# FFN1 of a recurrent block: the fetch of W1's blocks moves from SyncE's queue to ScalarE's, and VectorE's transpose of them to the head of its tile

## What is computed

```python
def quant_rows(a):
    scale = jnp.maximum(jnp.max(jnp.abs(a), axis=-1, keepdims=True) / 127.0, 1e-8)
    return jnp.clip(jnp.round(a / scale), -127.0, 127.0) * scale

def linear8bit(x, W, b):
    outlier = jnp.max(jnp.abs(x), axis=(0, 1)) > 3.0
    y = quant_rows(jnp.where(outlier, 0.0, x)) @ quant_rows(W).T
    return y + jnp.where(outlier, x, 0.0) @ W.T + b

xn = layernorm(x)                       # x: 4 x 512 x 512, f32
h = linear8bit(xn, W1, b1)              # W1: 2048 x 512
g = silu(linear8bit(h, W2, b2))         # W2: 512 x 2048
out = x + attention(xn) * g
```

## Time and profile before

| | |
|---|---|
| median of 3 runs | 801.87 us (799.75 to 803.87) |
| profiled execution, its own time | 802.13 us |
| span of its trace | 800.4 us |
| TensorE busy | 756.8 us, 95% |
| VectorE busy | 650.9 us, 81% |
| ScalarE busy | 395.4 us, 49% |
| GpSimd busy | 274.5 us, 34% |
| FFN1 in the trace | from 408.1 to 603.9 us |

### The profile page before, as it was taken

The page is one execution under the profiler, slowest core; times in us unless marked ns, Lnnn a source line. Parts: engine busy times, 40 slices in busy tenths (PEclk is TensorE's granted clock), DMA queues, the critical chain, the costliest instruction groups (busy, mean ns, idle before and its releaser), DMA issues. The chain is left out here.

```text
span 800.4 us, 11979 instructions
## 1 busy us (share of the span) xinstructions
PE 756.8 (95%) x4133; PEld 569.1 (71%) x4133; DVE 650.9 (81%) x1115; ACT 395.4 (49%) x670; POOL 274.5 (34%) x349
## 2 busy tenths in 40 slices
PE   5999999999999999999998998899997999999995
PEld 4878665556776767766576876688886788888884
DVE  7988999999999899995536585686868998599957
ACT  4354167767676667777633354355453333132212
POOL 7213135555555555554622112122200000036504
PEclk9999599999999999999999999999999999999999
DMA  7421303323222223334455857646332778436982
GB/s 265 146 106 53 81 21 89 82 81 95 82 83 83 82 82 100 88 108 134 158 184 141 253 149 180 171 99 149 77 71 73 270 216 263 165 106 219 307 315 105
DMA packets 115276, 110.71 MB, mean 138 GB/s; under 512 B 71808, under 2 KB 71824, under 8 KB 113680
## 3 DMA queue, kind: packets, MB, share of 16 engines
q1 hardware_dynamic: 115216, 109.95, 46.5%
HBM read 56.43 MB, written 40.37 MB: 121 GB/s over the span
## 5 line engine op out<-in xcount | busy, mean ns | idle before, releaser
L933 DVE TENSOR_REDUCE rowmax<-ps 128x2 f32<-128x512 f32 (+3 forms) x384 | 210.4, 591 | 19.6 <-PE ps L1010 18.0
L854 ACT ACTIVATE probs<-ps 128x512 f32<-128x512 f32 (+1 forms) x352 | 174.8, 558 | 71.3 <-PE ps L1023 70.0
L1010 PE MATMUL ps<-km,stack 128*128 128x256 f32 (+3 forms) x512 | 149.7, 347 | 2.2 <-PEq L195 1.9
L1023 PE MATMUL ps<-stack,ks 128*128 128x512 f32 (+1 forms) x352 | 131.4, 383 | 2.8 <-ACT probs L854 2.7
L1010 PEld LDWEIGHTS ps<-km,stack 128*128 128x128 f32 (+1 forms) x512 | 94.2, 197 | 43.2 <-DVE rowmax L933 23.8
L836 POOL TENSOR_SCALAR_AFFINE_SELECT probs<-probs 128x512 f32<-128x512 f32 x128 | 81.0, 641 | 78.3 <-ACT probs L854 77.1
L1861 PE MATMUL ps<-big_h 128*128 128x512 f32 x256 | 99.9, 390 | 2.0 <-issue 1.6
L1863 PE MATMUL ps<-big_h,big_l 128*128 128x512 f32 x256 | 99.6, 389 | 0.0
L1862 PE MATMUL ps<-big_l,big_h 128*128 128x512 f32 x256 | 99.6, 389 | 0.0
L1036 PE MATMUL ps<-probs,vones 128*32 128x512 f32 (+3 forms) x1024 | 82.2, 439 | 0.2 <-POOL probs L836 0.2
L1023 PEld LDWEIGHTS ps<-stack,ks 128*128 128x128 f32 x352 | 66.5, 189 | 11.7 <-ACT probs L854 6.2
(11 more groups left out here) (227 smaller groups left out, 1375.5 us busy)
## 6 DMA issues: line engine op xcount, KB each, us to landing
stack<-big_h SPq DMA_DIRECT2D x128, 64.0 KB, 2.0
h_scratch<-hs SPq DMA_DIRECT2D x7, 1024.0 KB, 4.5
hload<-h_scratch SPq DMA_DIRECT2D x14, 512.0 KB, 5.1
xn_scratch<-xa SPq DMA_DIRECT2D x4, 1024.0 KB, 4.4
stack<-big_l SPq DMA_DIRECT2D x64, 64.0 KB, 2.0
xi<-xn_scratch SPq DMA_DIRECT2D x16, 256.0 KB, 2.7
xe_scratch<-xm SPq DMA_DIRECT2D x16, 256.0 KB, 2.3
w2n<-in_L_ffn_W_dram SPq DMA_DIRECT2D x4, 1024.0 KB, 6.0
```

The costliest lines, as they stand in the source:

```text
L854: nc.scalar.activation(probs[p][:, o:o + nh * w], ps[:, STB[n % NST], 0:nh * w], ACT.Exp).then_inc(s_exp, 1)
L933: nc.vector.tensor_reduce(dst, src, AX_X, ALU.max).then_inc(s_red, 1)
L1010: last = nc.tensor.matmul(dst, stack[u % 3][rows, hp, P * qt:P * (qt + 1)], km[rows, u // KT, p0:p0 + npar, keys], start=True, stop=True)
L1023: ins = nc.tensor.matmul(ps[:, STB[n % NST], 0:nh * w].rearrange("p (h q) -> p h q", h=nh), ks[:, u // KT, p, P * kt:P * (kt + 1)], stack[ ...
```

## The change

Step 5 is issued from ScalarE's program instead of SyncE's: `load_w1_blocks(f + 2)` stands in tile f, behind the eviction of chunk 2 and ahead of that of chunk 3. (Before, SyncE had `load_w1_blocks(f + 1)` at the head of tile f.) Its waits stay the same. VectorE has step 6, `turn_w1(f + 1)`, as the first thing in tile f, ahead of `feature_max(f - 1)` and of step 2. In tile 0 step 2 for tile 2 moves ahead of `low_w1(1)`.

```diff
@@ SyncE @@
-                def load_w1_blocks(f):
-
-                    sp.wait_ge(s_w1k[f % 2], X_LOADED + 16 * (f // 2))
-                    if f > 2:
-                        sp.wait_ge(s_w1u, f - 2)
-                    for a in range(HB):
-                        rows = w1q_d[f % 2, :, :].rearrange("(b j) (k a i) -> a j k b i", b=HB, k=KT, a=HB)[a]
-                        sp.dma_start(w1x[SQ * a:SQ * (a + 1), :].rearrange("j (k b i) -> j k b i", k=KT, b=HB),
-                                     rows).then_inc(s_w1x, 16)
...
                 for f in range(FT):
-                    if 2 <= f + 1 < FT:
-                        load_w1_blocks(f + 1)
                     if f + 3 < FT:
                         load_w1(f + 3)
@@ ScalarE @@
+                def load_w1_blocks(f):
+
+                    act.wait_ge(s_w1k[f % 2], X_LOADED + 16 * (f // 2))
+                    if f > 2:
+                        act.wait_ge(s_w1u, f - 2)
+                    for a in range(HB):
+                        rows = w1q_d[f % 2, :, :].rearrange("(b j) (k a i) -> a j k b i", b=HB, k=KT, a=HB)[a]
+                        act.dma_start(w1x[SQ * a:SQ * (a + 1), :].rearrange("j (k b i) -> j k b i", k=KT, b=HB),
+                                     rows).then_inc(s_w1x, 16)
...
                         if c == 2 and f == 0:
                             high_w1(1)
+                        if c == 2 and f + 2 < FT:
+                            load_w1_blocks(f + 2)
@@ VectorE @@
                     if f == 0:
                         for i in range(EARLY, NT):
                             low_x(i)
+                        scale_w1(2)
                         low_w1(1)
+                    if 2 <= f + 1 < FT:
+                        turn_w1(f + 1)
                     if f:
                         feature_max(f - 1)
-                    if f + 2 < FT:
+                    if f and f + 2 < FT:
                         scale_w1(f + 2)
-                    if 2 <= f + 1 < FT:
-                        turn_w1(f + 1)
```

## The result

The changed kernel took 826.28 us, the median of four runs from 824.16 to 830.33, against 801.69 us before: a ratio of 1.0312, with a 95% interval from 1.0262 to 1.0362. The forecast was 824 us, slower. The profiled execution took 827.42 us, 25.3 more than the profiled one of before, and its span is 825.7 us. FFN1 goes from 408.6 to 629.3 us, 24.9 us longer than before; but for some tenths, the whole loss lies there.

A forecast was written before the change was run, and what follows sets the result against it. A ring longer than TensorE's 11.2 us tile bounds FFN1: from 422.75, thirteen passes of 12.85 us plus 14.2 of W2 traffic, then the last tiles, end FFN1 at 625.65, 21.7 us later: 824 us, range 805 to 843.

The forecast's parts named there:

- The ring: FFN1's loop of fetch, turn, feature maximum, scale, rounding, store, next fetch; one pass per tile, 12.85 us against TensorE's 11.2.
- The holes: TensorE's idle gaps in FFN1, waiting for W1's low part; forecast before nearly each tile through 13, also in 9 to 13.
- The ring without traffic: One pass with nothing beside the fetch: 8.5 us without the fetch, plus 4.35 for it, 12.85 us in all.
- The traffic: W2's stores and loads beside the fetch: 1.0 us in seven passes, 2.4 in three, nothing in three; sum 14.2 us.
- rival 4: Queues take turns: fetch issues wait for SyncE's, W2's load costs what both 1 MB transfers cost; 28 us, 838 us, chance 0.18.
- The end: Tile 14 starts 0.75 us before the last fetch at 604.0; two tiles of 11.2 us follow, FFN1 ends at 625.65.
- a lower clock: TensorE's slower matmuls after each hole, about 1.5 us; said to fall into the ring's slack, except once in tile 14.
- Rival 1: The holes go: TensorE runs 11.2 us tiles, 10.4 to 14 us less, about 790 us; chance 0.08.

## Why the prediction was right

**The mechanism.** The ring was read from the program's order and priced from rows of before; the chain after shows each of its steps. Undoing VectorE's half removes the loss, undoing ScalarE's does not, and 1.2 us more in the ring make the thirteen passes 13.0 us longer. The holes are fewer than forecast: seven, not one ahead of nearly each tile. Behind each of the five longest, 2.6 to 8.7 us, the tile runs at the lower clock at first and takes 12.6 to 13.7 us instead of 11.2, and the tile after it finds its low part ready.

**The ring without traffic.** Forecast 8.5 us without the fetch and 4.35 for it. Measured: 8.41 on the mean of 13 passes, and 4.37 for the fetch in two of the three tiles with no pieces of W2 (5.23 in the third). ScalarE's queue, then VectorE's turns, for a fetch beside W2's load (first row of each) and one beside nothing:

```profile
449.65 3.42 ACTq L1468 DMA_DIRECT2D w_blocks<-w_rounded_scratch  x4
...
468.84 2.63 ACTq L1468 DMA_DIRECT2D w_blocks<-w_rounded_scratch  x4
```

```profile
460.54 0.71 DVE L1558 STREAM_TRANSPOSE w1t_first<-w_blocks 128x512 f32<-128x512 f32 x1 [9.68 <-DMA w_blocks<-w_rounded_scratch]
473.21 0.71 DVE L1558 STREAM_TRANSPOSE w1t_second<-w_blocks 128x512 f32<-128x512 f32 x1 [4.28 <-DMA w_blocks<-w_rounded_scratch]
```

So the issue costs ScalarE what it cost SyncE (2.63 and 2.61 us), and the fetch is not shorter for its move. The Trainium skill ("DMA: Bandwidth & Descriptors", section "Issuing engines are not separate DMA queues") has all queues share the DMA engines; the trace agrees, with 4.37 us measured against 4.35 taken from SyncE's queue, and 7.2 to 10.9 us beside W2's load on the other queue.

**The traffic** is the term that was mis-sized, in both directions. For one or two pieces of W2 beside the fetch I took 1.0 us; seven passes measured 0.45 to 0.6. For W2's load I took 2.4 us, from a fetch in line behind it; the three measured 6.5, 2.8 and 3.8 us, in a queue beside it, the first of them above the upper bound of 4.5. Where I took nothing, one of three measured 0.9. The sum was 17.6 us instead of 14.2; that it is so near is luck in part, as the seven passes gave back 3.5 us of the 5.9 that the three cost more. Of rival 4 the half on W2's load was thus the nearer one (4.5), and the half on turns was not: the fetch's issues stayed at 2.64 us beside eight stores that took 4.93.

**The end** was 1.1 us later than the last fetch gave. Two terms did it together. I priced the low part at 1.27 us, and the one for tile 12 took 3.31 (first row; the last section has more on it), so TensorE starts that tile 2 us late, at 581.83. And I let a lower clock, at 1.5 us, fall into the ring's slack except in tile 14. Tile 12, behind a wait of 5.98 us, takes 13.7 us instead of 11.2; in the stretch where it starts the granted clock is 0.74. TensorE has no hole from there on. Tile 14's low part was ready at 605.60, and the tile starts at 606.75; with either term as forecast it would have started at about 605.7 (an estimate, from 11.2 us for tile 13).

```profile
578.47 3.31 POOL L1408 TENSOR_TENSOR w_low_first<-w1t_first,w_high_first 128x512 fp32r<-128x512 f32 x1
```

```profile
470.10 0.79 PE L1839 MATMUL ps<-big_h,w_high_first 128*128 128x512 f32 x1 [8.66 <-POOL w_low_first L1408]
...
581.83 0.79 PE L1839 MATMUL ps<-big_h,w_high_first 128*128 128x512 f32 x1 [5.98 <-POOL w_low_first L1408]
```

Together 25.3 us in the profiled execution, for 21.7 forecast.

**The rivals.** Rival 1, the holes gone, needed a fetch under 2.7 us; none was under 4.37. But its kernel exists: the change's queue with the old order took 793.8 us, where rival 1 said about 790.

## What to carry to other kernels

When a step that waits is moved ahead in an in-order program, follow what is queued behind it until the path ends or comes back: if it comes back, its length against the tile's length decides, and it is no use that each wait alone has a tile of room. A prefetch is only ahead if the data it fetches are made in an earlier tile than the one that it is issued in. And test the parts of a change one by one: here one half alone gained 1%, and the other alone lost 7.8%.

## What the runs showed of the hardware

GpSimd's low part, 128 x 512, took 1.27 to 1.31 us before and 3.31 in seven of its 14 places in the change, where it starts just behind VectorE's running maximum (GpSimd's row, then VectorE's, in the changed kernel):

```profile
434.07 3.31 POOL L1408 TENSOR_TENSOR w_low_first<-w1t_first,w_high_first 128x512 fp32r<-128x512 f32 x1
```

```profile
433.90 2.36 DVE L1608 TENSOR_TENSOR absmax<-absmax,habs 128x2048 f32<-128x2048 f32 x1
```

It ends 1.1 us after the maximum does, so it seems to wait for it. (Where the low part starts first, at 447.42, the maximum takes 2.96 us instead of 2.36.) The Trainium skill ("SBUF — State Buffer", section "Who interferes with whom") says that a VectorE instruction with two inputs in SBUF and a GpSimd instruction that reads SBUF block each other, and the later one waits; the trace agrees. It cost the ring nothing, as the low part is not in it. But TensorE waits for the low part, and the seven places of 3.31 us are just the tiles with the seven holes, so up to 2 us of each hole come from this.

DMA issues on ScalarE's queue did not wait for the instructions ahead of them. In the kernel with the old order and the longer turn:

```profile
444.64 2.00 ACT L1264 ACTIVATE habs<-hs,inl 128x2048 f32<-128x2048 f32 x1
445.69 1.25 ACTq L1469 DMA_DIRECT2D w_blocks<-w_rounded_scratch  x2
446.55 0.76 ACT L1489 ACTIVATE hs<-ps,b_col,w_scale 128x512 f32<-128x512 f32 x1
```

The fetch, which stands behind the eviction in the program, starts at 445.69, 0.86 us ahead of it, as soon as its own waits are met: the store that it waits for landed at 445.67. What stands behind the issues is held back. In the changed kernel the fourth eviction of tile 1 starts as the four issues end, after 5.25 us of idle time:

```profile
438.96 0.78 ACT L1488 ACTIVATE hs<-ps,b_col,w_scale 128x512 f32<-128x512 f32 x1 [5.25 <-issue]
```
